# Attention kernel on Trainium2: the output add divided between GpSimd and VectorE, scaling kept in PSUM for half of the rows, and two exponentials placed between copies on ScalarE

## What is computed

```python
xn = (x - moving_mean) * rsqrt(moving_var + 1e-3) * gamma + beta
q, k, v = xn @ Wq + bq, xn @ Wk + bk, xn @ Wv + bv
attn = softmax(q @ k.T * 64 ** -0.5, axis=-1)        # per row: 128 x 128
out = (attn @ v) @ Wo + bo
return xn + out
```

## Time and profile before

| | |
|---|---|
| median of three runs | 5316.65 us |
| profiled execution, its own time | 5315.75 us |
| span of that execution in the trace | 5313.9 us |
| TensorE clock granted in it | 0.999 of full |
| busy: TensorE, its weight loads, VectorE | 99%, 76%, 95% |
| busy: ScalarE, GpSimd | 90%, 69% |
| DMA | 806 MB, 152 GB/s, 78% of the 16 engines' time |

### The profile page before, as it was taken

How to read it: one execution, slowest core, us unless ns; L and a number is a source line. 1 busy time by engine, 2 the same in 40 slices (tenths; PEclk the granted TensorE clock), 3 DMA queues, 4 the chain that set the end, 5 groups by cost and what they waited for, 6 DMA issues and landing times. The chain is left out here.

```text
span 5313.9 us, 177339 instructions
## 1 busy us (share of the span) xinstructions
PE 5260.1 (99%) x51224; PEld 4017.8 (76%) x51224; DVE 5029.7 (95%) x15394; ACT 4772.2 (90%) x19460; POOL 3642.2 (69%) x2056
## 2 busy tenths in 40 slices
PE   7999999999999999999999999999999999999999
PEld 5777777777777777777777777777777777777777
DVE  7999999999999999999999999999999999999998
ACT  6999999999999999999999999999999999999998
POOL 5666666666666666666666666666666666666665
PEclk9999999999999999999999999999999999999999
DMA  6777777777777777777777777777777777777776
GB/s 132 153 153 152 153 153 153 153 153 153 153 153 152 153 153 153 153 153 154 153 153 153 153 153 153 153 153 153 153 153 153 153 153 153 153 153 153 153 152 129
DMA packets 4294236, 806.27 MB, mean 152 GB/s; under 512 B 4294208, under 2 KB 4294208, under 8 KB 4294208
## 3 DMA queue, kind: packets, MB, share of 16 engines
q1 hardware_dynamic: 4294208, 805.93, 78.1%
HBM read 537.10 MB, written 268.44 MB: 152 GB/s over the span
## 5 line engine op out<-in xcount | busy, mean ns | idle before, releaser
L252 POOL TENSOR_TENSOR x_weighted<-x_in,row_weights 128x1024 f32<-128x1024 f32 x1024 | 2425.5, 2369 | 1554.9 <-issue 1159.7
L300 ACT ACTIVATE probs<-score_ps,neg_top 128x128 f32<-128x128 f32 x8192 | 2876.6, 386 | 0.0
L385 DVE SCALAR_TENSOR_TENSOR y<-o_ps,inv_sum,x_scaled_rows 128x64 f32<-128x64 f32 x8192 | 1665.5, 276 | 218.2 <-DVE inv_sum L378 213.3
L300 ACT ACTIVATION_READ_ACCUMULATOR probs<-score_ps,neg_top 128x1 f32 x8192 | 1854.2, 226 | 0.0
L461 PE MATMUL probsT_ps<-ident,probs 128*128 128x128 f32 x8192 | 1286.8, 280 | 2.5 <-ACT probs L300 2.0
L257 POOL TENSOR_TENSOR x_scaled_rows<-x_weighted,out_bias 128x512 f32<-128x512 f32 x1024 | 1216.0, 1187 | 90.7 <-POOL x_weighted L252 20.2
L392 DVE TENSOR_REDUCE row_stat<-score_ps 128x8 f32<-128x1024 f32 x1024 | 1244.2, 1215 | 6.5 <-PE score_ps L474 6.5
L474 PE MATMUL score_ps<-xT,g 64*128 64x128 f32 x16384 | 1190.8, 285 | 1.9 <-ACT g L284 1.9
L485 PE MATMUL u_ps<-probsT,x_in 128*64 128x128 f32 x16384 | 1120.6, 279 | 0.0
L474 PEld LDWEIGHTS score_ps<-xT,g 64*128 64x128 f32 x16384 | 994.6, 187 | 128.0 <-ACT g L284 5.0
L501 PE MATMUL g_ps<-xT,w_g 128*128 128x512 f32 x2048 | 1051.0, 595 | 2.9 <-DVE xT L425 2.9
(11 more groups left out here) (65 smaller groups left out, 1332.1 us busy)
## 6 DMA issues: line engine op xcount, KB each, us to landing
x_quads<-in_x SPq DMA_DIRECT2D x4096, 64.0 KB, 2.2
x_in<-in_x SPq DMA_DIRECT2D x1024, 256.0 KB, 2.9
out<-y SPq DMA_DIRECT2D x1024, 256.0 KB, 2.7
norm_row<-in_L_conv_gamma SPq DMA_DIRECT2D x1, 32.0 KB, 3.7
norm_row<-in_L_conv_beta SPq DMA_DIRECT2D x1, 32.0 KB, 3.7
norm_row<-in_L_conv_moving_mean SPq DMA_DIRECT2D x1, 32.0 KB, 4.2
norm_row<-in_L_conv_moving_var SPq DMA_DIRECT2D x1, 32.0 KB, 4.3
norm_row<-in_L_conv_bo SPq DMA_DIRECT2D x1, 32.0 KB, 4.3
```

What stands on the lines that cost most here:

```text
L252: nc.gpsimd.tensor_tensor(x_weighted[:, n % 2, :, 0:2 * C].rearrange("p s (h c) -> p s h c", h=2), x_in[:, n % 8, :, None, :].broadcast_to ...
L300: last = nc.scalar.activation(probs[:, n % 2, q, :], score_ps[n % 2][:, q // PAIRS, q % PAIRS * W:(q % PAIRS + 1) * W], ACT.Exp, bias=neg_ ...
L385: last = nc.vector.scalar_tensor_tensor(y[:, s, q, :], o_rows[:, q, :], inv_sum[:, s, q:q + 1], x_scaled_rows[:, n % 8, q, :], ALU.mult, A ...
```

## The change

It has four parts.

1. **y divided.** VectorE now multiplies rows 0 to 3 of `o_ps` by the inverted sums into a new SBUF tile `attn` in one operation, and rows 4 to 7 in place in PSUM in another. GpSimd adds the residual to `attn` and writes the first half of y. VectorE adds the residual to the scaled rows 4 to 7 in `o_ps` and writes the second half. The eight row operations of L385 are gone. TensorE's first output product now waits for `attn_kept` and `y_half_found` of the group before, in place of `y_found`, and SyncE's store waits for both halves.
2. **VectorE's order.** The copy to `uT` comes after the two small reductions (it was in front of them), and the add of rows 4 to 7 comes right after the copy.
3. **The inversion** of the sums moves to the end of the step before (group t - 2 at the end of step t).
4. **ScalarE's order.** Exponential 0 of group t is put in front of the `g` copy and exponential 1 in front of the second copy of transposed tiles. Exponentials 2 to 7 stay behind it.

The diff, cut to its core:

```diff
         inv_sum = sb("inv_sum", [128, 4, GROUP])
+        attn = sb("attn", [128, 4, HALF, C])
         y = sb("y", [128, 4, GROUP, C])
...
         sum_inverted = sem_ring("sum_inverted")
+        attn_kept = sem_ring("attn_kept")
+        o_scaled = sem_ring("o_scaled")
+        y_half_found = sem_ring("y_half_found")
         x_weighed = sem_ring("x_weighed")
...
                 sp.wait_ge(y_found[parts(n)], uses(r, n))
+                sp.wait_ge(y_half_found[parts(n)], uses(r, n))
                 sp.dma_start(out_groups[group(r, n)], y[:, parts(n), :, :]).then_inc(y_stored[parts(n)], DMA_INC)
...
                         pool.wait_ge(y_found[s], uses(r, n - 8))
+                        pool.wait_ge(y_half_found[s], uses(r, n - 8))
                     nc.gpsimd.tensor_tensor(x_scaled_rows[:, n % 8], x_weighted[:, n % 2, :, 0:C], bias_b,
                                             ALU.add).then_inc(x_scaled[s], 1)
+                n = t - 3
+                if exists(r, n, peeled):
+                    s = parts(n)
+                    pool.wait_ge(attn_kept[s], uses(r, n))
+                    pool.wait_ge(x_scaled[s], uses(r, n))
+                    if exists(r, n - 4, peeled):
+                        pool.wait_ge(y_stored[s], dma_uses(r, n - 4))
+                    nc.gpsimd.tensor_tensor(y[:, s, 0:HALF, :], attn[:, s], x_scaled_rows[:, n % 8, 0:HALF, :], ALU.add).then_inc(y_found[s], 1)
 
...
 
+            def exponentials(r, n, peeled, rows):
+                if not exists(r, n, peeled):
+                    return
+                s = parts(n)
+                if 0 in rows:
+                    act.wait_ge(neg_top_found[s], uses(r, n))
+                    if exists(r, n - 2, peeled):
+                        act.wait_ge(probsT_b_made[parts(n - 2)], uses(r, n - 2))
+                    if exists(r, n - 4, peeled):
+                        act.wait_ge(sum_inverted[s], uses(r, n - 4))
+                for q in rows:
+                    last = nc.scalar.activation(probs[:, n % 2, q, :], score_ps[n % 2][:, q // PAIRS, q % PAIRS * W:(q % PAIRS + 1) * W],
+                                                ACT.Exp, bias=neg_top[:, s, q:q + 1], accum_out=prob_sum[:, s, q:q + 1])
+                    if q == HALF - 1:
+                        last.then_inc(probs_a_found[s], 1)
+                    if q == GROUP - 1:
+                        last.then_inc(probs_b_found[s], 1)
+
             def step(r, t, peeled):
...
                     nc.scalar.activation(probsT[:, n % 2, 0:HALF, :], probsT_rows, ACT.Copy).then_inc(probsT_a_kept[s], 1)
+                exponentials(r, t, peeled, range(0, 1))
                 n = t + 1
...
                                          ACT.Identity, bias=g_bias[:, 0:1]).then_inc(g_kept[s], 1)
+                exponentials(r, t, peeled, range(1, 2))
                 n = t - 1
...
                     nc.scalar.activation(probsT[:, n % 2, HALF:GROUP, :], probsT_rows, ACT.Copy).then_inc(probsT_b_kept[s], 1)
-                n = t
-                if exists(r, n, peeled):
-                    s = parts(n)
-                    act.wait_ge(neg_top_found[s], uses(r, n))
-                    if exists(r, n - 2, peeled):
-                        act.wait_ge(probsT_b_made[parts(n - 2)], uses(r, n - 2))
-                    if exists(r, n - 4, peeled):
-                        act.wait_ge(sum_inverted[s], uses(r, n - 4))
-                    for q in range(GROUP):
-                        last = nc.scalar.activation(probs[:, n % 2, q, :], score_ps[n % 2][:, q // PAIRS, q % PAIRS * W:(q % PAIRS + 1) * W],
-                                                    ACT.Exp, bias=neg_top[:, s, q:q + 1], accum_out=prob_sum[:, s, q:q + 1])
-                        if q == HALF - 1:
-                            last.then_inc(probs_a_found[s], 1)
-                    last.then_inc(probs_b_found[s], 1)
+                exponentials(r, t, peeled, range(2, GROUP))
 
...
                     s = parts(n)
-                    dve.wait_ge(probs_b_found[s], uses(r, n))
-                    nc.vector.reciprocal(inv_sum[:, s, :], prob_sum[:, s, :]).then_inc(sum_inverted[s], 1)
                     dve.wait_ge(sum_inverted[s], uses(r, n))
                     dve.wait_ge(o_made[s], uses(r, n))
-                    dve.wait_ge(x_scaled[s], uses(r, n))
                     if exists(r, n - 4, peeled):
-                        dve.wait_ge(y_stored[s], dma_uses(r, n - 4))
-                    for q in range(GROUP):
-                        last = nc.vector.scalar_tensor_tensor(y[:, s, q, :], o_rows[:, q, :], inv_sum[:, s, q:q + 1],
-                                                              x_scaled_rows[:, n % 8, q, :], ALU.mult, ALU.add)
-                    last.then_inc(y_found[s], 1)
+                        dve.wait_ge(y_found[s], uses(r, n - 4))
+                    nc.vector.tensor_tensor(attn[:, s], o_rows[:, 0:HALF, :], inv_sum[:, s, 0:HALF, None].broadcast_to([128, HALF, C]),
+                                            ALU.mult).then_inc(attn_kept[s], 1)
+                    nc.vector.tensor_tensor(o_rows[:, HALF:GROUP, :], o_rows[:, HALF:GROUP, :],
+                                            inv_sum[:, s, HALF:GROUP, None].broadcast_to([128, HALF, C]), ALU.mult).then_inc(o_scaled[s], 1)
                 n = t
...
                                             AX_X, ALU.max).then_inc(max_found[s], 1)
-                n = t - 2
-                if exists(r, n, peeled):
-                    s = parts(n)
-                    dve.wait_ge(u_made[s], uses(r, n))
-                    if exists(r, n - 2, peeled):
-                        dve.wait_ge(o_made[parts(n - 2)], uses(r, n - 2))
-                    nc.vector.tensor_copy(uT[:, n % 2], u_ps[:].rearrange("p (k w) -> p k w", k=PAIRS)) \
-                        .then_inc(u_kept[s], 1)
                 n = t
...
                                             ALU.add).then_inc(neg_top_found[s], 1)
+                n = t - 2
+                if exists(r, n, peeled):
+                    s = parts(n)
+                    dve.wait_ge(u_made[s], uses(r, n))
+                    if exists(r, n - 2, peeled):
+                        dve.wait_ge(o_made[parts(n - 2)], uses(r, n - 2))
+                    nc.vector.tensor_copy(uT[:, n % 2], u_ps[:].rearrange("p (k w) -> p k w", k=PAIRS)) \
+                        .then_inc(u_kept[s], 1)
+                n = t - 3
+                if exists(r, n, peeled):
+                    s = parts(n)
+                    dve.wait_ge(o_scaled[s], uses(r, n))
+                    dve.wait_ge(x_scaled[s], uses(r, n))
+                    if exists(r, n - 4, peeled):
+                        dve.wait_ge(y_stored[s], dma_uses(r, n - 4))
+                    nc.vector.tensor_tensor(y[:, s, HALF:GROUP, :], o_rows[:, HALF:GROUP, :], x_scaled_rows[:, n % 8, HALF:GROUP, :],
+                                            ALU.add).then_inc(y_half_found[s], 1)
                 n = t + 1
...
                                         x_quads[:, s].rearrange("p k w -> p (k w)")).then_inc(xT_kept[s], 1)
+                n = t - 2
+                if exists(r, n, peeled):
+                    s = parts(n)
+                    dve.wait_ge(probs_b_found[s], uses(r, n))
+                    nc.vector.reciprocal(inv_sum[:, s, :], prob_sum[:, s, :]).then_inc(sum_inverted[s], 1)
 
...
                     if exists(r, n - 1, peeled):
-                        pe.wait_ge(y_found[parts(n - 1)], uses(r, n - 1))
+                        pe.wait_ge(attn_kept[parts(n - 1)], uses(r, n - 1))
+                        pe.wait_ge(y_half_found[parts(n - 1)], uses(r, n - 1))
                     nc.tensor.matmul(o_pairs[:, :, 0, :], uT[:, n % 2, 0, :], w_o_all, start=True, stop=True)
```

## The result

The changed kernel takes 5602.02 us (median of four runs, 5601.51 to 5603.72). The kernel before took 5316.47 beside it. The ratio is 1.0538, 95% interval 1.052 to 1.0556, so the change makes the kernel 5.4% slower. The profiled execution took 5601.51 us with a span of 5599.7.

A forecast was written before the change was run, and what follows sets the result against it. The bound was a 5.10 us chain through VectorE's y, maxima and uT copy and TensorE's output products. The change's new cycle summed to 5.36: 1024 x 5.36 + 44 = 5533 span, 5535 us execution, range 5450 to 5650.

The forecast's parts named there:

- The cycle: Scores, maxima, small reductions, copy to uT, add, TensorE's first output product, next scores: a new closed chain of 5.36 us a step.
- eight terms: Parts of the new chain from scores to next scores: 1.21, 1.26, 0.20, 0.08, 0.60, 0.42, 0.06 and 1.53 us.
- The eighth term: From the end of VectorE's add of rows 4 to 7 to TensorE's first output product, put at 0.06 us.
- The add's price: VectorE's add of rows 4 to 7 from start to end, put at 0.42 us, between 0.34 and 0.85.
- the two products: VectorE's multiplications into attn and in place in PSUM, 0.34 us each, through at 0.84 after the scores' start.
- the cover: TensorE's scores hide VectorE's two multiplications, since the maxima cannot start before 1.21 us; without it they would cost 0.68.
- rival B: VectorE's multiplications cost over 0.52 us each and set the maxima's start: 5790 and 6108 us; chance 0.08.
- VectorE's own work: VectorE's work after the change, claimed to fall to roughly 4.4 us a step.
- TensorE's own pace of 5.09: TensorE alone was said to need 5.09 us a step, from the scores at 41.60 to those at 46.69.
- rival A: TensorE alone decides, the new wait is met in time: 5.09 us a step, 5258 us, 1.1% faster; chance 0.10.
- the 0.59: GpSimd's add for its half of y, 256 elements, put at 0.59 us, half of its 1.18 for 512.

The follow-up runs named there:

- the best kernel: Changed kernel with the product in place first, then the other product and the add, all before the maxima, copy to uT right behind the maxima: 5052.06 us.
- the last experiment: The best kernel with all of y on VectorE, both products in PSUM and both adds before the maxima: 5065.83 us, ratio 0.9528.

## Why the prediction was right, and where its sizes were off

**The cycle** came as forecast, and its place is shown twice. With the add moved to in front of the maxima the loss is gone, and with the bank released without moving the add it is gone as well. Of the eight terms seven measured within 0.01 of their estimate: 1.21, 1.26, 0.20, 0.09, 0.60, 0.41 and 1.52.

**The eighth term, "its hand-over to TensorE 0.06 (as from uT)"**, was mis-sized and measured 0.115. I took the figure from a hand-over in which the wait met last was not the last in the list. That is 0.055 x 1024 = 56 us of the 67 between 5535 and 5602. Turning the waits gives 0.045 of it back, which shows the cause. The other 11 us are what is left of the uneven steps (a mean of 5.429 against 5.41 in the rows is 19 us, mostly one step in eight that is 0.1 longer) after a start and end of 40 us rather than 44 and the rounding of the terms. The time lies inside the range of 5450 to 5650.

**The add's price** was right (0.42, measured 0.414), and so was that of the two products, the one with its output in PSUM included (0.42). They ended 0.92 after the scores' start. The maxima waited 0.28 for the scores, so the cover held and rival B has no part in it. One number beside the sum was too low: I put VectorE's own work at roughly 4.4 a step, and it is busy for 4.58 (4692.9 / 1024).

**TensorE's own pace of 5.09** was wrong, and with it rival A. I read it off a step between 41.60 and 46.69 in which I took TensorE to wait for nothing. The same trace, kernel before, shows the wait that I passed over:

```profile
44.66 0.66 ACT L277 ACTIVATE probsT<-probsT_ps 128x512 f32<-128x512 f32 x1
44.68 0.19 PEld L509 LDWEIGHTS o_ps<-w_o,uT 128*128 128x128 f32 x1 [0.28 <-DVE uT L401]
...
45.07 0.39 PE L509 MATMUL o_ps<-w_o,uT 128*128 128x128 f32 x2
...
45.46 0.63 PE L461 MATMUL probsT_ps<-ident,probs 128*128 128x128 f32 x4
...
2606.93 1.02 PE L501 MATMUL g_ps<-xT,w_g 128*128 128x512 f32 x2
```

The second transposes came 0.39 after the product and not 0.22. They go into the one bank that ScalarE's first copy was still reading until 45.32, and that copy had begun 0.4 before the product. Without these 0.17 the step is 4.92, close to the 4.89 of the best kernel. The kernel before was thus bound by the chain through VectorE alone, and 0.2 us a step were to be won by an earlier uT, as the kernels of 5052 and 5066 us show. For the change itself the error did not matter, because its cycle is longer than either pace. But rival A was put at 5258 where 5052 can be had, and two of my expectations inherited that.

**GpSimd** did become 78% busy, but with an add of 0.73 and not 0.59: the share came out right because the step was longer too. I had scaled the 0.59 from operations with one broadcast input, and this one has two full inputs. Whether that is the reason no run shows. It stayed hidden. **ScalarE's order** costs and brings nothing, as forecast, in both kernels. **The inversion** ended before the products could begin (0.50 idle behind it).

## What to carry to other kernels

When an operation is split or moved, look for the last reader of every buffer that is not doubled. Here one add of 0.41 us, put behind 2.1 us of other work, held a PSUM bank, and that hold with its longer hand-over cost 392 us. And before an engine's own pace is taken from a step, look at each start in that step for a wait, for the engine may look full because an input comes just as the previous work ends.

## What the runs showed of the hardware that I had not expected

- An input that comes 0.2 us earlier can shorten TensorE's step by 0.2 us. The copy to uT ended 0.91 after the start of g's matmuls in the kernel before and 0.70 after it in the last experiment, and the step went from 5.10 to 4.89 (where it ended after 0.80, to 4.99): the weights of a matmul are loaded under the matmuls in front of it, if its waits are met in time. Busy shares do not tell the two cases apart (99% in both).
- Where several waits stand in front of an instruction, the time from the signal to the start depends on their order. It is 0.115 us on TensorE when the last in the list is met last, and 0.07 when that one is followed by a wait already met. On VectorE it is 0.10 to 0.13 against 0.03 to 0.04.
- A wait whose value needs a register operation can cost as much. The 375 hand-overs of VectorE that take 0.12 to 0.13 in the better order are those in which such an operation stands between the signal and the start. That goes by the trace alone: no run takes the operation out.
- Of two adds that both read only SBUF, one on VectorE and one on GpSimd, the one that starts second is held: mostly 0.7 to 1.0 us in place of 0.41 on VectorE, 0.91 to 1.01 in place of 0.73 on GpSimd.
